# First attention: VectorE takes the maxima before the low part of q, the comparisons before the low part of o, and ScalarE normalises one step later

## The chip, the core and the metric

The kernel runs on one core of a Trainium2 chip. The metric is the device time of one execution in microseconds (us). It is a chain of four layers in one program; the change touches only the first.

## The reference, cut to what matters

Four sub-layers follow one another on x (2 batches of 2048 tokens, 512 wide). The first is a gated cross-attention with 16 heads of 32 over a context of 128 tokens; the second is a layer that runs on the 256 best-scored tokens of each batch.

```
x = x + tanh(g_xattn[0]) * L0_xattn(layernorm(x), ctx, ...)   # first attention: the change is here
x = x + tanh(g_ffn[0])   * L0_ffn(layernorm(x), ...)          # top 256 of 2048 tokens per batch, by x @ w_router
...
q = x @ Wq.T + bq;  att = softmax(q k^T * scale);  out = (att v) @ Wo.T + bo
```

## The kernel before

The first attention (tile names begin with `A_`) goes over 8 tiles of 512 tokens (`n` = 0 to 7). Each tile takes four slots `j` = 0 to 3, one for each group of four heads; a slot is numbered `s` = 4n + j, 0 to 31. Products are made in pairs of a high and a low half, for precision. The order of the work on each engine is written out by hand, and semaphores join the engines.

In slot s, TensorE makes the scores of group s (L982, L984) and the projection of q for the next tile (L914). It then makes the scores from which VectorE takes the maxima of the *next* group (`scores_for_max`, L925), the row sums (L996) and the product with V (`weigh`, L941). The first half of the output projection of the previous tile follows (L603), then the transposed maxima (`turn_maxima`, L932), the transposed router scores and the counts of the ranking (L614, L627), and the second half of the output projection (L603). The next slot's scores need the transposed maxima, copied by ScalarE (`keep_mT`, L825).

In the last slot of a tile (j = 3, while n + 2 < 8) TensorE also transposes x of tile n + 2 in four chunks (L905). ScalarE copies each chunk (`keep_xT`, L817 and L821) and GpSimd makes its low half (`low_x`, L771). The projection of q in the next slot waits for all four. Three conditions of the order matter here:

- In a slot with j = 3, n at least 1 and below 7, the output projection waits for the low half of q of that same slot, since it uses the same bank (`pe.wait_ge(q_ev, QT * (n + 2))` ahead of `project_out`).
- GpSimd's queue has, in such a slot, `low_x` of chunks 0 to 2, then `post_scales` (L515 to L521), which waits for the variance that VectorE's `add_out` (L650 to L657) leaves in this slot, and only then `low_x` of chunk 3 (L771).
- ScalarE's exponentials (L873) stand behind `high_o`, `add_gated` and whatever else the slot still has for ScalarE.

VectorE's slot has: low half of q (`keep_q_low`, L1050), `maxima` (L1089, L1094, L1096), the refined reciprocal of the row sums (L1112, L1114), the division (`divide`, L1101), the router score of a chunk (`score`, L666), the residual sum and its statistics (`add_out`), the low half of the output (`low_o`, L1106), in slots with j = 1 the statistics of x and with j = 2 its layer norm (L1034, L1044), and the comparisons that rank the chunk of six slots ago (`compare`, L678 and L684; the width grows by 128 with each chunk of a batch and starts again at 16).

Of the kernel before, what the change touches and what calls it, by code (L numbers as in the profile page):

```python
# [59 lines left out]
def need(eng, sem, value):  # L60

    if not (isinstance(value, int) and value <= 0):
        eng.wait_ge(sem, value)
# [76 lines left out]
def load_gates(eng, io, cst):  # L140

    for n, name in enumerate(("g_xattn", "g_ffn")):
        eng.dma_start(cst["gates_raw"][:, 2 * n:2 * n + 2],
                      io[name].rearrange("(a n) -> a n", a=1).to_broadcast([P, 2])).then_inc(cst["gates_loaded"], 16)


def make_gates(act, cst):

    act.wait_ge(cst["gates_loaded"], 32)
    act.activation(cst["gates"][:, :], cst["gates_raw"][:, :], ACT.Tanh).then_inc(cst["gates_tanh"], 1)  # L150
# [209 lines left out]
def narrow_attention(nc, io, cst, L, chosen):  # L360
# [8 lines left out]
    SLOTS = GROUPS * STEPS  # L369
    with stage_semaphores(nc, name) as sem, ExitStack() as ctx, ExitStack() as main:  # L370
# [101 lines left out]
        def chunk_at(s, lag):  # L472

            return s - lag if 0 <= s - lag < CHUNKS else None
# [20 lines left out]
        def found_slot(b):  # L495

            return hot_slots(b)[-1] + 1
# [36 lines left out]
        def normalise(act, s):  # L534

            q = chunk_at(s, ROUTE)
            if q is not None:
                (n, c), k = divmod(q, SUB), q + 1
                act.wait_ge(p_sh, 3 * k - 2)
                need(act, fin, k)  # L540
                if c == 0:
                    need(act, stored[n % 2], 32 * (n // 2))
                act.activation(N2[n % 2][:, c, :], R[n % 2][:, c, :], ACT.Identity, bias=shift[:, c:c + 1],
                               scale=rstd2[:, c:c + 1]).then_inc(p_xn, 1)
# [29 lines left out]
        def keep_found(act, s):  # L574

            for b in range(NB):
                if s == found_slot(b):
                    act.wait_ge(found, b + 1)
                    act.activation(idf[:, b, :, :], id_ps, ACT.Copy).then_inc(id_kept, 1)
# [79 lines left out]
        def score(dve, s):  # L659

            q = chunk_at(s, ROUTE)
            if q is not None:
                n, c = divmod(q, SUB)
                need(dve, p_sc, q)
                dve.wait_ge(p_xn, q + 1)
                dve.tensor_tensor_reduce(junk[:, :], N2[n % 2][:, c, :], wr[:, :], 1.0, 0.0, ALU.mult, ALU.add,  # L666
                                         own[:, q:q + 1]).then_inc(p_sc, 1)
# [144 lines left out]
        @block.scalar  # L812
        def _(act):
            def keep_xT(n, c):
                act.wait_ge(x_tr, SUB * n + c + 1)
                need(act, x_lo, SUB * n + c - 1)
                act.activation(xt[c % 2][:, :, :], TX[:, :, :], ACT.Copy).then_inc(x_te, 1)  # L817
                act.wait_ge(x_te, SUB * (n - 1) + c + 1)
                if c == 0:
                    need(act, q_mm, QT * n)  # L820
                act.activation(xh[:, :, c * P:(c + 1) * P], xt[c % 2][:, :, :], ACT.Copy).then_inc(x_hi, 1)  # L821

            def keep_mT(k):
                act.wait_ge(m_tr, k + 1)
                act.activation(mT[:, :], mps, ACT.Copy).then_inc(m_te, 1)  # L825

            def keep_q(n, m, bank=PJ):
                act.wait_ge(q_mm, QT * n + m + 1)
                act.activation(qh[:, m, :], bank[:, :], ACT.Identity, bias=bq[:, m:m + 1]).then_inc(q_hi, 1)

            def guess_rz(k):

                need(act, o_div, k - 1)
                act.wait_ge(z_mm, k)
                act.activation(rz[:, :], ZB[:, :], ACT.Ln).then_inc(z_ln, 1)
                act.wait_ge(z_ln, k)
                act.activation(rz[:, :], rz[:, :], ACT.Exp, scale=-1.0).then_inc(z_ex, 1)

            load_gates(act, io, cst)
            make_gates(act, cst)  # L840
            act.preload_act_table_set("natural_log_exp_and_others")
            act.wait_ge(w_in, 32)
            for k in range(KD):
                act.activation(wqh[:, k, :], wq[:, k, :], ACT.Copy).then_inc(wq_hi, 1)
            for c in range(SUB):
                act.wait_ge(x_tr, c + 1)
                act.activation(xh[:, :, c * P:(c + 1) * P], first_turns[c], ACT.Copy).then_inc(x_hi, 1)
            stage.keep_k(act)
            stage.high_k(act)
            for m in range(QT):  # L850
                keep_q(0, m, first_banks[m % 3])
            for c in range(SUB):
                keep_xT(1, c)
                if c == 2:
                    keep_mT(0)

            def scale_wo(k):
                act.wait_ge(cst["gates_tanh"], 1)
                act.wait_ge(b_in, 48)
                act.activation(wo[:, k, :], wo[:, k, :], ACT.Copy, scale=tg).then_inc(wo_sc, 1)  # L860
                act.wait_ge(wo_sc, k + 1)
                act.activation(woh[:, k, :], wo[:, k, :], ACT.Copy).then_inc(wo_hi, 1)

            def high_o(s):
                act.wait_ge(o_div, s + 1)
                act.activation(oh[s // GROUPS % 2][:, s % GROUPS, :], OB[:, :], ACT.Copy).then_inc(o_hi, 1)

            for s in range(SLOTS):
                n, j = divmod(s, GROUPS)
                last = n == STEPS - 1  # L870
                for g in range(HG):
                    act.wait_ge(s_mm, HG * s + g + 1)
                    act.activation(pr[:, g, :], SC[:, g, :], ACT.Exp, scale=scale).then_inc(s_ex, 1)  # L873
                if not last:
                    keep_q(n + 1, j)
                guess_rz(s + 1)
                normalise(act, s)
                turn_x = j == GROUPS - 1 and n + 2 < STEPS
                if turn_x:
                    keep_xT(n + 2, 0)  # L880
                    keep_xT(n + 2, 1)
                if s + 1 < SLOTS:
                    keep_mT(s + 1)
                keep_row(act, s)
                keep_sums(act, s)
                high_o(s)
                keep_found(act, s)
                if turn_x:
                    keep_xT(n + 2, 2)
                    keep_xT(n + 2, 3)  # L890
                add_gated(act, s)
                if n == 0:
                    scale_wo(j)
# [135 lines left out]
        def _(dve):  # L1029
# [56 lines left out]
            def maxima(k):  # L1086

                dve.wait_ge(m_mm, k + 1)
                dve.tensor_reduce(mx[:, :, :], SC[:, :, :].rearrange("p g (c x) -> p c g x", x=CTX),  # L1089
                                  AX.X, ALU.max).then_inc(m_mx, 1)  # L1090
                dve.wait_ge(m_mx, k + 1)
                need(dve, m_tr, k)
                m = by_slot(m2[:, :, :])
                dve.tensor_copy(m[:, :, :, 0], mx[:, :, :]).then_inc(m_hi, 1)  # L1094
                dve.wait_ge(m_hi, k + 1)
                dve.tensor_tensor(m[:, :, :, 1], mx[:, :, :], m[:, :, :, 0], ALU.subtract).then_inc(m_lo, 1)  # L1096

            def divide(s):

                dve.wait_ge(pv, s + 1)  # L1100
                dve.tensor_tensor(OB[:, :], OB[:, :], rz[:, :], ALU.mult).then_inc(o_div, 1)  # L1101

            def low_o(s):

                dve.wait_ge(o_hi, s + 1)
                dve.tensor_tensor(ol[s // GROUPS % 2][:, s % GROUPS, :], OB[:, :],  # L1106
                                  oh[s // GROUPS % 2][:, s % GROUPS, :].bitcast(F32), ALU.subtract).then_inc(o_ok, 1)
# [16 lines left out]
            for s in range(SLOTS):  # L1124
                n, j = divmod(s, GROUPS)
                last = n == STEPS - 1
                if not last:
                    keep_q_low(n + 1, j)
                if s + 1 < SLOTS:
                    maxima(s + 1)  # L1130
                refine_rz(s + 1)
                dve.wait_ge(z_r, s + 1)
                divide(s)
                score(dve, s)
                add_out(dve, s)
                low_o(s)
                if n + 2 < STEPS and j == 1:
                    ln_stats(n + 2)
                if n + 2 < STEPS and j == 2:
                    ln_apply(n + 2)  # L1140
                compare(dve, s)
                choose(dve, s)

        main.close()  # L1144
# [2023 lines left out]
```

## Time and profile before

| what | value |
| --- | --- |
| median of 3 runs | 1783.61 us (1780.41 to 1787.19) |
| the profiled execution | 1779.8 us, span 1777.9 us |
| mean granted TensorE clock | 0.937 of full speed |
| busy: TensorE, VectorE, ScalarE, GpSimd | 87%, 73%, 51%, 32% of the span |
| first attention | about 20 us to 476 us of the span |

A row of the timeline gives start, duration, engine, line, operation, output and input, and in brackets how long the engine had been idle and what released it.

### The profile page before, as it was taken

The page shows a single profiled execution, that of the slowest core. Times are in us where ns is not written, and L with a number is a line of the kernel's source. Part 1 is how long each engine was busy: PE and PEld are TensorE (multiplying, and loading weights), DVE is VectorE, ACT ScalarE, POOL GpSimd, SP SyncE. Part 2 cuts the span into 40 slices and gives each one's busy share as a digit, 9 for nine tenths or more (in the row PEclk, how much of TensorE's full clock was granted, in tenths as well). Part 3 has the DMA queues.
Part 4 walks back from the last instruction along what each step waited for, and adds up shares of the span by engine and source line. Part 5 has one row for each costly group of instructions (what it writes and reads, how often), then busy time and mean ns, then how long its engine had stood idle before and what let it go on. Part 6 is the DMA issues. An engine that isn't in the chain of part 4 may idle for free. (4 is left out here: it accounts for less than half of the span.)

```text
span 1777.9 us, 25990 instructions
## 1 busy us (share of the span) xinstructions
PE 1544.6 (87%) x9654; PEld 982.3 (55%) x9687; DVE 1300.4 (73%) x2098; ACT 907.4 (51%) x1467; POOL 570.6 (32%) x560
## 2 busy tenths in 40 slices
PE   7788888997678979968999999999997778888887
PEld 5455555554456648745666665666664444554453
DVE  5677788888542546654776775777766599999997
ACT  3556665565544426426334333433433477777774
POOL 3233333123310002113112021112200297777771
PEclk9899999899888889989999999999999999999998
DMA  4112212222722424531020101102011330222111
GB/s 162 48 48 95 95 54 67 72 72 96 277 70 98 180 87 142 201 113 48 1 84 25 60 29 56 60 24 84 1 60 36 120 124 9 69 78 72 67 64 55
DMA packets 73284, 142.36 MB, mean 80 GB/s; under 512 B 8417, under 2 KB 17781, under 8 KB 72906
## 3 DMA queue, kind: packets, MB, share of 16 engines
q1 hardware_dynamic: 71914, 137.55, 22.5%
q0 software_dynamic: 960, 3.15, 0.6%
q8 instruction: 81, 1.33, 0.3%
q14 instruction: 41, 0.34, 0.1%
q10 hardware_dynamic: 288, 0.00, 0.0%
HBM read 97.67 MB, written 43.01 MB: 79 GB/s over the span
## 5 line engine op out<-in xcount | busy, mean ns | idle before, releaser
L2937 POOL TENSOR_TENSOR E_y<-E_y,E_centre 128x1024 f32<-128x1024 f32 x64 | 151.6, 2368 | 6.7 <-ACT E_y L2966 3.7
L1492 ACT ACTIVATE D_oT<-D_OB 128x512 fp32r<-128x512 f32 x64 | 38.3, 599 | 221.0 <-DVE D_OB L1809 221.0
L2929 POOL TENSOR_SCALAR E_centre<-E_hs,E_cw,E_cb 128x512 f32<-128x512 f32 x64 | 108.8, 1700 | 53.4 <-DVE E_hs L3025 53.3
L2825 PE MATMUL E_HP<-E_xT,E_w1q 128*128 128x512 bf16 x482 | 123.9, 398 | 2.4 <-ACT E_xT L2943 0.4
L1781 DVE TENSOR_TENSOR D_q_low<-D_PJ,D_q_high 128x512 fp32r<-128x512 f32 x60 | 41.5, 692 | 97.1 <-ACT D_q_high L1468 97.1
L2850 PE MATMUL E_YT<-ident,E_y 128*128 128x128 f32 x496 | 70.4, 289 | 42.1 <-DVE E_am L3043 38.1
L3034 DVE SCALAR_TENSOR_TENSOR E_y<-E_hs,E_cw,E_y 128x512 f32<-128x512 f32 x128 | 105.4, 862 | 0.0
L2838 PE MATMUL E_OP<-E_w2q,E_yb 128*128 128x512 bf16 x446 | 102.8, 384 | 0.7 <-issue 0.7
L1561 PE MATMUL D_PJ<-D_xT_high,D_wq_high 128*128 128x512 f32 x240 | 101.2, 422 | 0.1
L1561 PE MATMUL D_PJ<-D_xT_high,D_wq_low 128*128 128x512 f32 x240 | 94.7, 395 | 0.0
L1561 PE MATMUL D_PJ<-D_xT_low,D_wq_high 128*128 128x512 f32 x240 | 94.0, 392 | 0.0
L2850 PEld LDWEIGHTS E_YT<-ident,E_y 128*128 128x128 f32 x496 | 60.0, 149 | 58.1 <-issue 41.9
L1569 PE MATMUL D_ZB<-D_wo_high,D_oT 128*128 128x512 f32 x240 | 82.8, 406 | 2.8 <-DVE D_rz L1823 2.8
L2825 PEld LDWEIGHTS E_HP<-E_xT,E_w1q 128*128 128x128 bf16 x512 | 50.3, 102 | 56.4 <-issue 9.7
L1569 PE MATMUL D_PJ<-D_wo_high,D_oT 128*128 128x512 f32 x240 | 80.8, 397 | 0.0
L3025 DVE TENSOR_TENSOR E_hs<-E_HP,E_rs 128x1024 f32<-128x1024 f32 x64 | 77.4, 1209 | 2.7 <-PE E_HP L2825 2.7
L603 PE MATMUL A_TX<-A_wo_high,A_oT 128*128 128x512 f32 x176 | 71.0, 446 | 6.7 <-PEq L1144 6.7
L1791 DVE TENSOR_REDUCE D_mx<-D_SC 128x16 f32<-128x2048 f32 x32 | 73.1, 2284 | 4.1 <-PE D_SC L1582 4.1
L3043 DVE TENSOR_REDUCE E_am<-E_YT 128x4 f32<-128x1024 f32 x62 | 75.2, 1213 | 1.2
L2956 ACT ACTIVATE E_centre<-E_hs,E_cw 128x512 f32<-128x512 f32 x64 | 46.1, 721 | 58.7 <-DVE E_hs L3025 56.8
L914 PE MATMUL A_PJ<-A_xT_high,A_wq_high 128*128 128x512 f32 x120 | 56.6, 472 | 20.6 <-POOL A_xT_low L771 15.4
L1815 DVE TENSOR_TENSOR D_oT<-D_OB,D_oT 128x512 fp32r<-128x512 f32 x64 | 44.2, 691 | 41.0 <-ACT D_oT L1492 41.0
(445 smaller groups left out, 4270.2 us busy)
## 6 DMA issues: line engine op xcount, KB each, us to landing
A_res<-in_x SPq DMA_DIRECT2D x8, 1024.0 KB, 5.4
xn_d<-A_xn SPq DMA_DIRECT2D x8, 1024.0 KB, 4.4
x_d<-A_res SPq DMA_DIRECT2D x8, 1024.0 KB, 4.3
W_raw<-in_w1T SPq DMA_DIRECT2D x16, 512.0 KB, 3.6
W_raw<-in_w2T SPq DMA_DIRECT2D x16, 512.0 KB, 3.8
D_res<-x_d SPq DMA_DIRECT2D x8, 1024.0 KB, 6.0
x_d<-D_res SPq DMA_DIRECT2D x8, 1024.0 KB, 4.5
E_res<-x_d SPq DMA_DIRECT2D x8, 1024.0 KB, 5.5
```

Of the source, the lines that this page charges most:

```text
L603: mm = pe.matmul(out_bank(n, c), o[:, k, c * P:(c + 1) * P], w[:, k, :], start=k == 0 and o is h and w is woh, stop=k == QT - 1 and o is l)
L1561: mm = pe.matmul(bank[:, :], w[:, k, m * P:(m + 1) * P], x[:, k, :], start=k == 0 and x is xh and w is wqh, stop=k == KD - 1 and x is xl)
L1569: mm = pe.matmul(bank, o[i][:, k, c * P:(c + 1) * P], w[half][:, k, :], start=k == 0 and o is oh and w is woh, stop=k == OT - 1 and o is ol)
L1791: dve.tensor_reduce(mx[:, :, :], SC[:, :, :].rearrange("p g (c x) -> p c g x", x=CTX), AX.X, ALU.max).then_inc(m_mx, 1)
L2825: mm = pe.matmul(HP[:, i % 2, e, :], w1q[:, k, m * P:(m + 1) * P], XT[n % 2][:, k, :], start=k == 0, stop=k == KD - 1)
L2838: mm = pe.matmul(out_bank(n, c), yb[:, k, c * P:(c + 1) * P], w2q[:, k, :], start=k == 0, stop=k == MC - 1)
L2850: mm = pe.transpose(turn_bank(i)[:, c, e, :], Y[i // MP % 2][:, 2 * (i % MP) + e, c * P:(c + 1) * P], ident[:, :])
L2929: pool.tensor_scalar(U[i % 2][:, 0, :], hs[i % NBUF][:, 0, 1:TILE + 1], cw[:, 2 * p, 1:2], cb[:, 2 * p:2 * p + 1], ALU.mult, ALU.add).then ...
L2937: pool.tensor_tensor(y, y, U[i % 2][:, :, :], ALU.add).then_inc(t0, 1)
L3025: dve.tensor_tensor(hs[i % NBUF][:, :, 1:TILE + 1], HP[:, i % 2, :, :], RS[n % 2][:, :].rearrange("p (a t) -> p a t", a=1).to_broadcast([P ...
L3034: dve.scalar_tensor_tensor(out=Y[n % 2][:, m, :], in0=hs[i % NBUF][:, e, 2:TILE + 2], scalar=cw[:, m, 2:3], in1=Y[n % 2][:, m, :], op0=ALU ...
L3043: dve.tensor_reduce(am[:, :, i % MP], turn_bank(i).rearrange("p c e x -> p c (e x)"), AX.X, ALU.max, apply_absolute_value=True).then_inc(a ...
```

## The change

Nothing is computed differently; four steps change place within a slot. On VectorE `maxima` comes ahead of `keep_q_low`, and `compare` and `low_o` come directly behind `divide`, ahead of `score` and `add_out`. On ScalarE `normalise` (L543), which stood behind the reciprocal's guess, comes behind `high_o`.

```diff
@@ ScalarE, slot s
                 guess_rz(s + 1)
-                normalise(act, s)
                 turn_x = j == GROUPS - 1 and n + 2 < STEPS
                 if turn_x:
                     keep_xT(n + 2, 0)
...
                 high_o(s)
+                normalise(act, s)
                 keep_found(act, s)
@@ VectorE, slot s
+                if s + 1 < SLOTS:
+                    maxima(s + 1)
                 if not last:
                     keep_q_low(n + 1, j)
-                if s + 1 < SLOTS:
-                    maxima(s + 1)
                 refine_rz(s + 1)
                 dve.wait_ge(z_r, s + 1)
                 divide(s)
+                compare(dve, s)
+                low_o(s)
                 score(dve, s)
                 add_out(dve, s)
-                low_o(s)
...
-                compare(dve, s)
                 choose(dve, s)
```

VectorE's instructions in slot 19 (n = 4, j = 3), before; `A_q_low` is the low half of q, `A_SC` the scores, `A_OB` the output before its projection, `A_oT` its halves, `A_res` the residual, `A_lower` the comparisons:

```order
L1050 SCALAR_TENSOR_TENSOR A_q_low<-A_PJ,A_bq,A_q_high 128x512
L1089 TENSOR_REDUCE A_mx<-A_SC 128x16
...
L1101 TENSOR_TENSOR A_OB<-A_OB,A_rz 128x512
L666 ISA A_junk,A_own_scores<-A_xn_1,A_w_router 128x512
L666 ISA A_own_scores 128x1
L650 TENSOR_TENSOR A_res<-A_PJ,A_res 128x512
L652 BN_STATS A_stats<-A_res 128x6
L655 BN_AGGR A_mv<-A_stats 128x2
L657 TENSOR_SCALAR A_var<-A_mv 128x1
L1106 TENSOR_TENSOR A_oT<-A_OB,A_oT 128x512
L678 SCALAR_TENSOR_TENSOR A_ties_at,A_ties<-A_scores_row,A_own_scores,A_following 128x128
L684 TENSOR_SCALAR A_lower,A_less<-A_scores_row,A_own_scores 128x1792
```

The same slot in the changed kernel:

```order
L1089 TENSOR_REDUCE A_mx<-A_SC 128x16
L1094 CAST A_m<-A_mx 128x16
L1096 TENSOR_TENSOR A_m<-A_mx,A_m 128x16
L1050 SCALAR_TENSOR_TENSOR A_q_low<-A_PJ,A_bq,A_q_high 128x512
...
L1101 TENSOR_TENSOR A_OB<-A_OB,A_rz 128x512
L678 SCALAR_TENSOR_TENSOR A_ties_at,A_ties<-A_scores_row,A_own_scores,A_following 128x128
L684 TENSOR_SCALAR A_lower,A_less<-A_scores_row,A_own_scores 128x1792
L1106 TENSOR_TENSOR A_oT<-A_OB,A_oT 128x512
L666 ISA A_junk,A_own_scores<-A_xn_1,A_w_router 128x512
L666 ISA A_own_scores 128x1
L650 TENSOR_TENSOR A_res<-A_PJ,A_res 128x512
...
L657 TENSOR_SCALAR A_var<-A_mv 128x1
```

The low half of q now stands behind three instructions of the maxima, and the variance (L657) behind both comparisons and the low half of the output.

ScalarE's instructions of slot 20 in the changed kernel, from the reciprocal's guess to the exponentials of the next slot; before, L543 stood between L837 and L825:

```order
L835 ACTIVATE A_rz<-A_ZB 128x512
L837 ACTIVATE A_rz<-A_rz 128x512
L825 ACTIVATE A_mT<-A_SC 128x512
L563 ACTIVATE A_scores_row<-A_SC 128x128
L572 ACTIVATE A_later<-A_SC 128x13
L866 ACTIVATE A_oT<-A_OB 128x512
L543 ACTIVATE A_xn_1<-A_res,A_shift,A_rstd 128x512
L554 ACTIVATE A_res<-A_res,A_offset,A_gain 128x512
L873 ACTIVATE A_probs<-A_SC 128x512 x4
```

The normalisation now stands between the division's result and the exponentials.

## Rows read from the trace of the kernel before

**Rows 1.** Groups of TensorE, 40 to 455 us: busy, mean ns, idle before by releaser.
```profile
L914 PE MATMUL A_PJ<-A_xT_high,A_wq_high 128*128 128x512 f32 x112 | 52.7, 470 | 17.8 <-POOL A_xT_low L771 15.4 <-issue 2.4
...
L932 PE MATMUL A_SC<-identb,A_m 128*128 128x128 bf16 x128 | 13.1, 227 | 22.2 <-DVE A_m L1096 22.2
```

**Rows 2.** Timeline of slots 16 and 17.
```profile
258.95 2.28 DVE L1089 TENSOR_REDUCE A_mx<-A_SC 128x16 f32<-128x2048 f32 x1
...
263.09 0.70 DVE L1101 TENSOR_TENSOR A_OB<-A_OB,A_rz 128x512 f32<-128x512 f32 x1
...
265.13 2.06 ACT L873 ACTIVATE A_probs<-A_SC 128x512 f32<-128x512 f32 x4
...
268.03 0.67 PE L925 MATMUL A_SC<-A_k_high,A_q_high 32*128 32x128 f32 x16
...
268.86 0.75 DVE L1050 SCALAR_TENSOR_TENSOR A_q_low<-A_PJ,A_bq,A_q_high 128x512 fp32r<-128x512 f32 x1 [0.27 <-ACT A_q_high L829]
...
269.53 2.28 DVE L1089 TENSOR_REDUCE A_mx<-A_SC 128x16 f32<-128x2048 f32 x1
...
270.99 0.80 ACT L543 ACTIVATE A_xn<-A_res,A_shift,A_rstd 128x512 f32<-128x512 f32 x1
```

**Rows 3.** Timeline of slot 0, the first tile.
```profile
53.63 0.40 PE L932 MATMUL A_SC<-identb,A_m 128*128 128x128 bf16 x4 [1.88 <-DVE A_m L1096]
...
57.43 2.04 ACT L873 ACTIVATE A_probs<-A_SC 128x512 f32<-128x512 f32 x4
...
60.37 0.67 PE L925 MATMUL A_SC<-A_k_high,A_q_high 32*128 32x128 f32 x16
```

**Rows 4.** Timeline of slot 18 and the start of slot 19.
```profile
285.71 0.40 PE L932 MATMUL A_SC<-identb,A_m 128*128 128x128 bf16 x4 [2.93 <-DVE A_m L1096]
...
292.79 1.38 DVE L678 SCALAR_TENSOR_TENSOR A_ties_at<-A_scores_row,A_own_scores,A_following 128x128 bf16<-128x128 f32 x1
...
295.97 0.74 DVE L1050 SCALAR_TENSOR_TENSOR A_q_low<-A_PJ,A_bq,A_q_high 128x512 fp32r<-128x512 f32 x1
```

**Rows 5.** Timeline of slot 19, up to the projection of slot 20.
```profile
298.31 0.47 PE L603 MATMUL A_PJ<-A_wo_high,A_oT 128*128 128x512 f32 x1
...
298.94 0.94 DVE L1094 CAST A_m<-A_mx 128x16 bf16<-128x16 f32 x1
...
300.20 0.40 PE L932 MATMUL A_SC<-identb,A_m 128*128 128x128 bf16 x4 [0.25 <-DVE A_m L1096]
...
301.13 0.27 ACT L563 ACTIVATE A_scores_row<-A_SC 128x128 f32<-128x128 f32 x1
...
302.91 0.69 DVE L650 TENSOR_TENSOR A_res<-A_PJ,A_res 128x512 f32<-128x512 f32 x1
...
304.58 0.15 DVE L657 TENSOR_SCALAR A_var<-A_mv 128x1 f32<-128x1 f32 x1
...
305.30 0.72 POOL L515 TENSOR_TENSOR A_rstd<-A_var,minus_half 128x1 f32<-128x1 f32 x1
...
305.52 2.07 DVE L684 TENSOR_SCALAR_CACHE_REDUCE A_lower<-A_scores_row,A_own_scores 128x1792 bf16<-128x1792 f32 x1
...
308.37 0.76 PE L914 MATMUL A_PJ<-A_xT_high,A_wq_high 128*128 128x512 f32 x1 [3.14 <-POOL A_xT_low L771]
```

**Rows 6.** Timeline of slot 23: the comparisons at their second smallest width.
```profile
362.82 0.47 DVE L684 TENSOR_SCALAR_CACHE_REDUCE A_lower<-A_scores_row,A_own_scores 128x256 bf16<-128x256 f32 x1
```

**Rows 7.** Stretches of the projection in slots 16 and 20: PEclk is the column before the last two.
```profile
254.40:258.20 3.80, 3.70 (x32) 2.85 (x36) 0.00 (x0) 0.64 (x1) 2.34 (x2) 1.00 0.19 67
308.30:314.80 6.50, 6.43 (x32) 4.77 (x36) 0.22 (x1) 0.69 (x1) 2.28 (x2) 0.53 0.09 34
```

**Rows 8.** Timeline of slot 27 (n = 6, j = 3).
```profile
403.72 0.74 DVE L1050 SCALAR_TENSOR_TENSOR A_q_low<-A_PJ,A_bq,A_q_high 128x512 fp32r<-128x512 f32 x1
...
404.51 0.50 PE L603 MATMUL A_PJ<-A_wo_high,A_oT 128*128 128x512 f32 x1 [1.15 <-DVE A_q_low L1050]
...
407.21 0.40 PE L932 MATMUL A_SC<-identb,A_m 128*128 128x128 bf16 x4 [1.03 <-DVE A_m L1096]
```

## The prediction

> **What bounds the kernel now.** The profiled execution took 1779.8 us. The change touches only the first attention, some 455 us of it, so I read that stretch alone: first the groups of TensorE, then the timeline of each kind of slot.
>
> The groups show what there is to win. TensorE waits 22.2 us in all for VectorE's maxima ahead of the transposes L932, and 15.4 us (about 3.1 us in each of five tiles) for GpSimd's low half of x ahead of the projection L914 [rows 1]. The first is what the change aims at, and 22.2 us its ceiling. The second is what it may lengthen.
>
> Three kinds of slot must be told apart.
>
> *Slots with j = 0 or 1* form a loop. The reader is to see in the timeline that from the division (263.09) to the exponentials (265.13) pass 2.04 us, that the exponentials end at 267.19, and that TensorE takes up its next scores only at 268.03: ScalarE has 0.84 us to spare, TensorE's own queue ends last [rows 2]. The maxima start at 269.53, 10.58 us after those of the slot before (258.95).
>
> *Slots with j = 2* follow the layer norm's statistics. VectorE is late, and TensorE waits 2.93 us for the maxima in slot 18 [rows 4].
>
> *Slots with j = 3* end in a chain: maxima, score row, residual and variance on VectorE (L657 at 304.58), GpSimd's scales (L515 at 305.30), its last low half of x, and the projection at 308.37, for which TensorE waited 3.14 us [rows 5].
>
> **The change, part by part.**
>
> *Maxima ahead of the low half of q.* Before, the maxima wait for q low, which starts at 268.86 and is followed by them 0.67 us later [rows 2]; now they start as soon as the scores are there (268.03 + 0.67, about 268.75). So the maxima come 0.75 us earlier, and low q comes behind them, some 2.8 us later. The division behind both stays where it was, since VectorE does the same work before it.
>
> In the first tile TensorE waits 1.88 us for the maxima and its next scores (60.37) come 0.9 us after the exponentials (57.43 + 2.04) [rows 3]. Moving the first by 0.75 us brings in about 0.65 us a slot before the exponentials decide. Three slots (0 to 2): **-1.9 us**. Bounds: 0 and -2.3 us.
>
> In slots with j = 2, TensorE's wait of 2.93 us shrinks by the same 0.75 us [rows 4]. This head start I carry into the slot with j = 3, which follows, and count it there.
>
> *Normalise behind high o.* It takes 0.80 us [rows 2] and now stands between the division and the exponentials. The loop from division to division becomes 2.04 + 0.80 to the exponentials, 2.06 for them, 0.1 to the next scores, 0.67 for these, 0.07 to the maxima, 4.14 from maxima to division (258.95 to 263.09), and 0.72 for low q, which is now in between: 10.60 us against 10.58 [rows 2]. So what L932 waits no longer (0.2 us) isn't won: ScalarE's spare time is used up. The slots with j = 0 or 1 and those of tile 6 that were shorter than 10.6 us (I count seven, by 0.1 to 0.35 us) come up to it: **+1.0 us**, bounds 0 and +2.
>
> In the last tile there is no projection, and the exponentials stand close behind ScalarE's work; in each of its four slots the 0.80 us may show. Mostly TensorE's scores come later than that. I take **+0.5 us**, bounds 0 and 3.2 (4 x 0.80).
>
> *Slot 27, tile 6.* Here TensorE already waits 1.15 us for low q (403.72 to 404.46) ahead of the output projection (404.51), and then 1.03 us for the maxima (407.21) [rows 8]. Now the maxima start at 403.72 and end 2.75 us later, low q another 0.75 us: 407.25, so the projection starts 2.75 us later. It takes 407.21 - 404.51 - 1.03 = 1.67 us, and L932 comes at 408.95, **+1.7 us**. Bounds: +1.0 and +2.8, the whole delay.
>
> *Slots with j = 3 in tiles 1 to 5.* I work slot 19 out [rows 4, 5]. The maxima take low q's place at 295.97, less 1.0 us: the comparison that took 1.38 us at 292.79 is now done far earlier, beside an idle GpSimd, and should take some 0.4. That is 295.0, a choice. They end after 3.5 us (295.97 + 0.67 to 300.15 before, with a cast of 0.94 us among them) at 298.5, low q at 299.3. The output projection starts at 299.35, not 298.31. Before, it took 300.20 - 298.31 - 0.25 = 1.64 us: L932 at 301.0, +0.8 us. The head start of slot 18 is gone.
>
> The score row, which the comparisons need, came 0.93 + 0.27 us after L932: now 302.2. Comparisons: 2.07 us and 0.3 for the ties: 304.55. Low o and score, each taken at the 0.69 us of L650, which has their shape, 128x512: 305.95. The residual and its statistics, 302.91 to 304.73 before, 1.82 us: 307.8. From L515 to the projection passed 308.37 - 305.30 = 3.07 us: 310.9. The projection is **2.5 us later** than at 308.37. Low o cost 0.7 of this, the comparisons 2.35, and they had slack only of 0.6 (304.73 to 305.30).
>
> In the other four tiles only the comparisons' width differs: 0.47 us at 256 columns [rows 6], 2.07 at 1792 [rows 5], so in between 1.0 at 768 and 1.54 at 1280. By this, slots 15, 11, 7 and 23 lose 2.0, 1.4, 0.9 and 0.9, with slot 19 7.7 us. In slots 7 and 23 VectorE isn't behind, so the head start survives: I take **+5.8 us** in all. Bounds: 2.5 (slot 19 alone) and 7.7.
>
> The cast L1094 took 0.94 us while GpSimd was making low halves of x, for 16 columns [rows 5]. [...]
>
> *The clock.* A projection of 12 matmuls behind the pause of 3.1 us ran in slot 16 at the full 2.4 GHz (granted 1.00; stretch of 3.8 us with the scores) and in slot 20 nearly all at 1.2 GHz (granted 0.53; 6.5 us) [rows 7]. Longer pauses make the second likelier. In slot 16 alone up to 2.7 us are at stake; I take **+1.0 us**, bounds 0 and 8.
>
> **Sum.** -1.9 + 1.0 + 0.5 + 1.7 + 5.8 + 1.0 = +8.1 us: 1787.9 us against 1779.8 of the profiled execution. The median of the runs is 3.8 us above that, which gives 1791.7. I say 1791. A difference under 0.5% (8.9 us) is about what a measurement of this kernel can't tell from none.
>
> The statistics, last in the slot, cost nothing in slots with j = 0 to 2: the variance feeds a normalisation two slots later, and the residual is wanted by TensorE only after its next row sums, over 4 us after L650 before. If that cover went, the price would be the same 2 to 3 us a slot. The stores behind normalise on SP's queue come some 4 us later; the residual they make room for is added a slot and a half later.
>
> **Rivals.**
>
> *Within 0.5%, a small loss*, as above: 1791 us, its own range 1783 to 1792. Chance 0.50.
>
> *The pauses grow and the clock falls with them.* Place: the projections of slots 8, 12, 16, 20 and 24 behind GpSimd, which wait 4.5 to 5.5 us and not 3.1. If each then runs wholly at 1.2 GHz and the clock stays there into the slot, every tile pays 1.5 us more: 7.7 + 5 x 1.5 + the rest (1.3) = +16.5, 1800 us. It decides from about +0.2 us a tile above my sum. For it: four of the five after such a pause already fell in part. Against it: those can't fall twice. [...] Chance 0.42, with the cases where the loops lose more than taken.
>
> *The head start counts everywhere.* The low q isn't waited for since TensorE comes later there than I say, and the variance comes in time. Then 0.75 us in three first slots and five with j = 2, and 0.2 us in some ten others: -8 us, 1776 us. For it: 22.2 us of waiting on maxima. Against it: slot 27 shows the wait for low q already. Half of this case and all beyond it make up 0.08 for faster by over 0.5%; what is left is within 0.5% and counted there.
>
> **Range.** 1780 to 1801: from the lower bounds (with a part of the third case) to the second case. Faster 0.08, same 0.50, slower 0.42.
>
> **What would show it.** In the changed profile TensorE's wait on VectorE ahead of L932 falls from 22.2 to below 15 us; a new wait of L603 on A_q_low appears in slots with j = 3, and of 1 to 4 us in slot 27; TensorE's wait on GpSimd ahead of L914 rises from 15.4 to above 20 us, and GpSimd's L515 there waits on L657. The loops of j = 0 and 1 come to 10.6 us. If L914's wait stays at 15 us, the term of 5.8 is wrong, and the kernel is as fast as before or faster. If L657 is in time but the clock differs, the term of the clock is.

## The result, and the profile after

The changed kernel takes 1805.13 us (median of 4 runs, 1803.19 to 1807.14), the kernel before beside it 1785.4 us (4 runs, 1780.41 to 1787.32): ratio 1.0115, interval 1.009 to 1.014. It is slower by some 20 us, beyond the predicted 1791 us and beyond the range's 1801. The profiled execution took 1803.19 us, against 1779.8.

The groups of TensorE over the first attention in the changed kernel (same stretch and columns as [rows 1]):

```profile
L914 PE MATMUL A_PJ<-A_xT_high,A_wq_high 128*128 128x512 f32 x112 | 52.1, 465 | 21.0 <-POOL A_xT_low L771 19.1 <-issue 1.9
...
L603 PE MATMUL A_PJ<-A_wo_high,A_oT 128*128 128x512 f32 x48 | 22.0, 504 | 11.6 <-DVE A_q_low L1050 11.6
...
L925 PE MATMUL A_SC<-A_k_high,A_q_high 32*128 32x128 f32 x496 | 21.3, 289 | 14.2 <-ACT A_probs L873 14.0
...
L932 PE MATMUL A_SC<-identb,A_m 128*128 128x128 bf16 x128 | 13.9, 236 | 14.6 <-DVE A_m L1096 14.6
```

The row of L925 in the kernel before, where it had not mattered:

```profile
L925 PE MATMUL A_SC<-A_k_high,A_q_high 32*128 32x128 f32 x496 | 22.1, 297 | 6.4 <-ACT A_probs L873 6.4
```

The wait for the maxima fell from 22.2 to 14.6 us. In its place stand 11.6 us of a wait for low q ahead of the output projection (1.1 us before), and 3.7 us more for GpSimd's low x ahead of the projection of q (15.4 to 19.1). TensorE also waits 7.6 us more for the exponentials (6.4 to 14.0). This last wait comes with `normalise`: it is 11.5 to 15.9 us in every experiment that moves it (e4, e6, e8, e10, e11) and 6.4 to 7.0 us in those that don't. What was won at one wait is more than paid at the others.

Slot 19, timeline of the changed kernel, from the maxima to the projection of slot 20 (answers to [rows 5]):

```profile
300.71 2.29 DVE L1089 TENSOR_REDUCE A_mx<-A_SC 128x16 f32<-128x2048 f32 x1
...
303.04 0.71 DVE L1094 CAST A_m<-A_mx 128x16 bf16<-128x16 f32 x1
...
303.78 1.21 DVE L1096 TENSOR_TENSOR A_m<-A_mx,A_m 128x16 bf16<-128x16 f32 x1
...
304.87 0.74 DVE L1050 SCALAR_TENSOR_TENSOR A_q_low<-A_PJ,A_bq,A_q_high 128x512 fp32r<-128x512 f32 x1
...
305.67 0.80 PE L603 MATMUL A_PJ<-A_wo_high,A_oT 128*128 128x512 f32 x1 [2.30 <-DVE A_q_low L1050]
...
306.26 0.63 PE L603 MATMUL A_PJ<-A_wo_low,A_oT 128*128 128x512 f32 x1
...
306.98 0.70 DVE L1101 TENSOR_TENSOR A_OB<-A_OB,A_rz 128x512 f32<-128x512 f32 x1
...
308.40 0.65 PE L932 MATMUL A_SC<-identb,A_m 128*128 128x128 bf16 x4
...
309.88 0.35 DVE L678 SCALAR_TENSOR_TENSOR A_ties_at<-A_scores_row,A_own_scores,A_following 128x128 bf16<-128x128 f32 x1 [2.21 <-ACT A_scores_row L563]
...
310.16 2.08 DVE L684 TENSOR_SCALAR_CACHE_REDUCE A_lower<-A_scores_row,A_own_scores 128x1792 bf16<-128x1792 f32 x1
...
312.33 1.27 POOL L771 TENSOR_TENSOR A_xT_low<-A_xT,A_xT_high 128x512 fp32r<-128x512 f32 x1 [6.20 <-ACT A_xT_high L821]
...
314.08 0.68 DVE L650 TENSOR_TENSOR A_res<-A_PJ,A_res 128x512 f32<-128x512 f32 x1
...
315.98 0.57 POOL L515 TENSOR_TENSOR A_rstd<-A_var,minus_half 128x1 f32<-128x1 f32 x1 [2.37 <-DVE A_var L657]
...
318.89 0.77 PE L914 MATMUL A_PJ<-A_xT_high,A_wq_high 128*128 128x512 f32 x1 [4.74 <-POOL A_xT_low L771]
```

The reader is to see a chain with no slack in it. The output projection stands 2.30 us for low q. It then runs at half clock (0.63 us a matmul, and a granted clock of 0.50 from 305.67 to 308.40, against 0.39 us and 1.00 from 298.31 to 300.20 before) and puts the maxima's transposes, the score row and the comparisons off; VectorE itself stands 2.21 us for that row. Only behind the comparisons comes the residual with its variance, for which GpSimd stands 2.37 us, and TensorE stands 4.74 us for GpSimd. From the maxima to the projection pass 18.2 us; before it was 308.37 - 296.64 = 11.7 (low q ended 0.67 us behind 295.97).

GpSimd's work beside the maxima of that slot:

```profile
301.17 2.51 POOL L805 TENSOR_TENSOR A_res<-A_res,A_bo 128x512 f32<-128x512 f32 x2
303.65 2.48 POOL L771 TENSOR_TENSOR A_xT_low<-A_xT,A_xT_high 128x512 fp32r<-128x512 f32 x2
```

Slot 15 ends in the same way, and the projection behind its pause now runs at half clock too, with its matmuls starting 0.43 us apart. Timeline:

```profile
258.54 0.77 PE L914 MATMUL A_PJ<-A_xT_high,A_wq_high 128*128 128x512 f32 x1 [4.16 <-POOL A_xT_low L771]
259.11 0.63 PE L914 MATMUL A_PJ<-A_xT_high,A_wq_low 128*128 128x512 f32 x1
...
263.93 0.71 PE L925 MATMUL A_SC<-A_k_high,A_q_high 32*128 32x128 f32 x16
```

and that stretch with slot 20's as windows (PEclk is the third number from the end):

```profile
258.54:264.64 6.10, 6.10 (x32) 4.41 (x36) 0.00 (x0) 0.60 (x1) 2.21 (x2) 0.55 0.01 3
318.89:325.60 6.71, 6.71 (x44) 4.21 (x44) 1.57 (x1) 1.19 (x2) 2.19 (x2) 0.76 0.01 2
```

The granted clock of slot 16's projection was 1.00 before and is 0.55 [rows 7]: 5.4 us to the next scores instead of 3.0. Before, its matmuls start 0.23 us apart, and those of slot 20's projection, granted 0.53, 0.43 us apart. The record has shares of full speed, 1.00 and 0.50; they are what the prediction and the expectations call 2.4 and 1.2 GHz. The same two marks before:

```profile
254.50 0.47 PE L914 MATMUL A_PJ<-A_xT_high,A_wq_high 128*128 128x512 f32 x1 [3.07 <-POOL A_xT_low L771]
...
257.46 0.67 PE L925 MATMUL A_SC<-A_k_high,A_q_high 32*128 32x128 f32 x16
```

The end of the slots, which are one block of the program. Behind it comes the first attention's closing part (the last output projections and the rest of the ranking), which starts on TensorE and ScalarE together. Changed kernel:

```profile
467.85 0.15 DVE L657 TENSOR_SCALAR A_var<-A_mv 128x1 f32<-128x1 f32 x1
468.08 0.57 POOL L515 TENSOR_TENSOR A_rstd<-A_var,minus_half 128x1 f32<-128x1 f32 x1 [5.96 <-DVE A_var L657]
...
469.48 2.48 POOL L805 TENSOR_TENSOR A_res<-A_res,A_bo 128x512 f32<-128x512 f32 x2
472.69 0.81 ACT L543 ACTIVATE A_xn<-A_res,A_shift,A_rstd 128x512 f32<-128x512 f32 x1 [7.34 <-PEq L1144]
```

Kernel before:

```profile
448.65 0.70 DVE L1101 TENSOR_TENSOR A_OB<-A_OB,A_rz 128x512 f32<-128x512 f32 x1
...
451.71 0.15 DVE L657 TENSOR_SCALAR A_var<-A_mv 128x1 f32<-128x1 f32 x1
...
453.34 2.48 POOL L805 TENSOR_TENSOR A_res<-A_res,A_bo 128x512 f32<-128x512 f32 x2
...
456.56 0.81 ACT L543 ACTIVATE A_xn<-A_res,A_shift,A_rstd 128x512 f32<-128x512 f32 x1 [5.88 <-PEq L1144]
```

The closing part's first work starts less than 1 us behind GpSimd's last bias (469.48 + 2.48 and 453.34 + 2.48), which stands behind the variance of slot 31. Division to variance took 3.1 us before, and takes 6.2 now (the division is at 461.61): +3.2 us, for TensorE and ScalarE alike.

**Where the 23.4 us of the two profiled executions lie.** The division (L1101) is VectorE's fixed mark in each slot. From its rows, changed less before, with two experiments beside it (below: e5 is the order of before compiled anew, e4 has the edits only in slots with j < 3 of tiles 0 to 6):

| stretch | predicted | changed | e5 | e4 |
| --- | --- | --- | --- | --- |
| division 0 to 3 | -1.9 | -2.2 | +0.4 | -2.0 |
| steps out of slots 3, 7, ... 23 (j = 3) | | +14.9 | -1.7 | +3.5 |
| other steps from 4 to 27 | | -6.2 | -0.6 | -9.6 |
| the last two together | +7.8 | +8.7 | -2.2 | -6.0 |
| 27 to 28 | +1.7 | +1.9 | +0.5 | -1.0 |
| 28 to 31, last tile | +0.5 | +4.3 | +4.1 | +0.3 |
| 31 to the block's end | 0 | +3.2 | +1.6 | +0.6 |
| behind the block, code untouched | 0 | +7.3 | -1.6 | +5.5 |

Single profiles carry several us of their own: with no edit at all the last tile is 4.1 us longer in e5, and the untouched code behind the block differs by -1.6 to +11.4 us among the twelve experiments. So sizes are taken from the timed comparisons, and the profiles say where to look.

### The profile page after: what moved, and what is told of

The parts are those of the page before. It is cut to its first block and busy times, and to the rows that moved or that the text cites. A ratio compares the mean times of both kernels' runs of the same rounds, so it can differ in the third digit from the quotient of the medians.

```text
span 1801.3 us, 26023 instructions
## 1 busy us (share of the span) xinstructions
PE 1558.4 (87%) x9687; PEld 989.1 (55%) x9687; DVE 1296.6 (72%) x2098; ACT 905.4 (50%) x1467; POOL 568.8 (32%) x560
## 5 line engine op out<-in xcount | busy, mean ns | idle before, releaser
L2825 PE MATMUL E_HP<-E_xT,E_w1q 128*128 128x512 bf16 x512 | 129.5, 399 | 0.4 <-ACT E_xT L2943 0.2
L1089 DVE TENSOR_REDUCE A_mx<-A_SC 128x16 f32<-128x2048 f32 x32 | 73.2, 2289 | 65.5 <-PE A_SC L925 65.4
L515 POOL TENSOR_TENSOR A_rstd<-A_var,minus_half 128x1 f32<-128x1 f32 x32 | 21.4, 668 | 187.2 <-DVE A_var L657 187.0
L603 PE MATMUL A_TX<-A_wo_high,A_oT 128*128 128x512 f32 x176 | 69.8, 439 | 8.2 <-PEq L1144 8.2
L914 PE MATMUL A_PJ<-A_xT_high,A_wq_high 128*128 128x512 f32 x120 | 55.8, 465 | 23.4 <-POOL A_xT_low L771 19.1
```

Source lines behind the costliest of these rows:

```text
L2825: mm = pe.matmul(HP[:, i % 2, e, :], w1q[:, k, m * P:(m + 1) * P], XT[n % 2][:, k, :], start=k == 0, stop=k == KD - 1)
```

## The experiments

All ratios are to the kernel before on the same chip, with 95% intervals; the microseconds of a loss or gain are worked out from the ratio. 0.1% is 1.8 us. The experiments' line numbers are shifted by up to three. Their code carries the three edits under conditions; the diffs show what results.

**e1, the maxima alone.**

```diff
+                if s + 1 < SLOTS:
+                    maxima(s + 1)
                 if not last:
                     keep_q_low(n + 1, j)
-                if s + 1 < SLOTS:
-                    maxima(s + 1)
```

> Only the maxima ahead of the low half of q; all else as before. Theory P (a delayed producer in the slots with j = 3): the head start of 0.75 us is kept in slots 0 to 2 and in the slots with j = 2 (about -2.7 and -3 us), and in six slots with j = 3 TensorE waits for low q ahead of the output projection (about 11 us of waiting in the changed kernel), which gives back more than it: the kernel lands between -3 and +6 us of the one before. Theory S (ScalarE's loop: the normalisation between division and exponentials is what costs): without it the head start is pure gain, -5 to -8 us. Theory K (TensorE's clock alone): the wait for low q brings more stretches at 1.2 GHz and +5 us or more.

1790.35 us, 1.0043 [1.0024, 1.0063]. Groups of TensorE:

```profile
L917 PE MATMUL A_PJ<-A_xT_high,A_wq_high 128*128 128x512 f32 x112 | 53.2, 475 | 19.0 <-POOL A_xT_low L771 16.2 <-issue 2.9
L603 PE MATMUL A_PJ<-A_wo_high,A_oT 128*128 128x512 f32 x56 | 26.0, 508 | 14.7 <-DVE A_q_low L1053 14.7
L935 PE MATMUL A_SC<-identb,A_m 128*128 128x128 bf16 x128 | 13.7, 233 | 15.4 <-DVE A_m L1099 15.4
```

The edit that should win costs 7.7 us by itself, a little more than the highest I had named. It brings the wait for low q (14.7 us) and hardly touches that for GpSimd (16.2). It rules out theory S; theory K, which had +5 us or more, fits it as well as P does, and is taken up behind the experiments.

**e2, comparisons and low o alone.**

```diff
                 divide(s)
+                compare(dve, s)
+                low_o(s)
                 score(dve, s)
                 add_out(dve, s)
-                low_o(s)
...
-                compare(dve, s)
```

> Only the comparisons and low o directly behind the division, ahead of the router score and the residual's statistics. Theory P: the variance reaches GpSimd 1 to 3 us later in five slots with j = 3 and in slot 31, where the block's end waits for GpSimd's last bias: 8 to 15 us slower than before, TensorE's wait for GpSimd ahead of the projection above 20 us against 15.4. Theory S: no change, within 2 us. Theory K: about +3 us.

1793.27 us, 1.007 [1.0049, 1.009]. Its group of the projection:

```profile
L917 PE MATMUL A_PJ<-A_xT_high,A_wq_high 128*128 128x512 f32 x112 | 51.7, 462 | 26.0 <-POOL A_xT_low L771 24.1 <-issue 2.0
```

The wait for GpSimd rose from 15.4 to 24.1 us, and nothing else is new. The loss, 12.5 us, is what theory P had (8 to 15). The losses of e1 and e2 add to 1.13%, and the changed kernel's is 1.15%.

**e3, both, with the normalisation at its old place** (e1 and e2's diffs).

> The changed kernel with ScalarE's normalisation put back to its old place. Theory P: the loss stays above 13 of the 20 us, and only the last tile, where the exponentials end the wait, gets back some 4 us. Theory S: most of the loss is gone, within 5 us of the kernel before.

1801.02 us, 1.0085 [1.0054, 1.0116]. Its lower end, 9.6 us, is above the 5 us of theory S, and its upper end holds the whole loss. By the medians moving `normalise` costs 0.3%, which these intervals don't tell from nothing.

**e4, all three edits, but only in slots with j < 3 of tiles 0 to 6.**

```diff
+                if s + 1 < SLOTS and (j < 3 and not last):
+                    maxima(s + 1)
...
+                if j < 3 and not last:
+                    compare(dve, s)
+                    low_o(s)
```

> All three edits in slots with j = 0 to 2 of tiles 0 to 6 only; slots with j = 3 and the last tile as before. Theory P: the losers are gone and the head starts of slots 0 to 2 and of j = 2 are kept, -3 to -6 us against the kernel before, 1778 to 1783 us. Theory S: the loops with j = 0 and 1 still have the normalisation in them and the loss stays in part, +3 us or more. Theory K: within 2 us of before.

1774.89 us, 0.9968 [0.9953, 0.9982]: faster than before. No listed group waits for low q, that for the maxima is 16.6 us, that for GpSimd 16.0. So the whole loss lies in slots with j = 3 and in the last tile.

**e5, no edit**: the order of before, with the conditions all off.

> No edit: the order of the kernel before, compiled once more, for a second profile of it. Every theory: ratio 1.000 within 0.002. What it is for: if TensorE's clock in the last tile is a matter of where the chip's changes of clock happen to fall, this profile may show slots 28 to 31 at another granted clock than 0.94, and the first attention up to 4 us longer or shorter, with nothing changed.

1781.51 us, 1.0008 [0.9991, 1.0025]. Windows of the last tile (division 28 to 31), PEclk third from the end; before:

```profile
419.23:448.65 29.42, 22.98 (x205) 12.65 (x204) 24.94 (x51) 18.46 (x38) 10.57 (x18) 0.94 0.42 143
```

e5:

```profile
417.99:451.46 33.47, 27.06 (x198) 13.67 (x197) 25.09 (x50) 18.04 (x36) 10.55 (x18) 0.80 0.38 127
```

e3, which has two of the edits there:

```profile
429.74:458.55 28.81, 22.39 (x197) 12.13 (x196) 25.07 (x50) 18.20 (x38) 10.08 (x18) 0.94 0.43 145
```

The same instructions in the same order take 29.4 or 33.5 us, with the granted clock at 0.94 or 0.80. The changed kernel's tile (33.7 us at 0.80) is of the second kind. Its +4.3 us are therefore no effect of the edits that this profile can show.

**e6, the changed kernel with slot 31 in the old order** (condition `s < SLOTS - 1` on the comparisons, low o and the normalisation).

> The changed kernel with slot 31 alone in the old order (comparisons behind the statistics, normalisation early). Theory P: the time from the last division to the end of the block falls back by about 3 us (11.0 to 7.8), and the kernel is 3 us faster than the changed one: ratio 1.010 to the one before. Rivals S and K: no change, 1.0115.

1796.57 us, 1.0086 [1.006, 1.0113]. End of the block:

```profile
463.07 0.70 DVE L1104 TENSOR_TENSOR A_OB<-A_OB,A_rz 128x512 f32<-128x512 f32 x1
...
467.03 0.15 DVE L657 TENSOR_SCALAR A_var<-A_mv 128x1 f32<-128x1 f32 x1
...
471.87 0.81 ACT L543 ACTIVATE A_xn<-A_res,A_shift,A_rstd 128x512 f32<-128x512 f32 x1 [6.65 <-PEq L1154]
```

From division to variance pass 4.0 us instead of 6.2, and the block ends 2.3 us sooner behind its last division (8.8 against 11.1). The time agrees with 2 to 5 us, though the intervals of the two kernels overlap.

**e7, the maxima first only where j < 3** (e1 with that condition).

> Only the maxima first, and only in slots with j = 0 to 2; comparisons, low o and normalisation as before. Theory P: the waits on low q are gone and the head starts kept: -2 to -5 us, about as good as all three edits in these slots. Rival C: the comparisons ahead of the statistics are what helped there; then this one is within 1 us of the kernel before.

1776.47 us, 0.9976 [0.9958, 0.9994]. The wait for low q is 1.8 us. The gain is e4's within the intervals, so it is the maxima that win in these slots, and the other two edits add nothing there that the timed runs show. Against e1, the maxima in the seven slots with j = 3 and a next tile cost 0.67%, 12 us: the largest piece of the loss.

**e8, the changed kernel with low q ahead of the maxima where j = 3.**

```diff
-                if s + 1 < SLOTS:
+                if s + 1 < SLOTS and j < 3:
                     maxima(s + 1)
                 if not last:
                     keep_q_low(n + 1, j)
+                if s + 1 < SLOTS and j == 3:
+                    maxima(s + 1)
```

> The changed kernel with low q back ahead of the maxima in the slots with j = 3. Theory P: TensorE's wait for low q (11.6 us) falls to about 1 us, what remains is the late variance and the block's end: 7 to 10 us of the 20 come back, ratio 1.006 to 1.008. Rival (all of the loss is the variance): ratio stays above 1.010.

1789.05 us, 1.004 [1.002, 1.0059]. This one line takes back 0.75%, 13 us, of the changed kernel's loss, somewhat more than I forecast, and agrees with e1 against e7. No listed group waits for low q any more.

**e9, before, with GpSimd's last low half of x ahead of its scales.** Nothing else in GpSimd's queue is altered.

```diff
                     if c == SUB - 1 and ahead:
-                        for i in range(SUB - 1):
+                        for i in range(SUB):
                             low_x(n + 2, i)
                     if n:
                         post_scales(pool, n - 1, c)
-                    if c == SUB - 1 and ahead:
-                        low_x(n + 2, SUB - 1)
```

> The kernel before, with one edit on GpSimd: the low half of x chunk 3 ahead of the scales of the previous tile's last chunk, so that the projection no longer waits behind VectorE's variance. Theory P: in each of five tiles the 1.5 us of the scales leave the path, TensorE's wait for GpSimd falls from 15.4 to about 8 us: 5 to 10 us faster, ratio 0.994 to 0.997. Rival (ScalarE's copies of x end last anyway): within 1 us.

1771.62 us, 0.9925 [0.9906, 0.9945]. The kernel gains 13 us, more than the 5 to 10 I forecast. The wait for GpSimd falls from 15.4 to 8.8 us:

```profile
L912 PE MATMUL A_PJ<-A_xT_high,A_wq_high 128*128 128x512 f32 x112 | 50.8, 453 | 11.2 <-POOL A_xT_low L771 8.8 <-issue 2.4
```

**e10, the changed kernel with the same edit.**

> The same GpSimd edit on the changed kernel. Theory P: the late variance no longer reaches the projection. Of the 20 us lost, what the comparisons cost in slots with j = 3 (some 8 us) and the 5 to 10 us of the edit itself come back; the wait on low q (about 8 us with its slow clock) and the 2.5 us at the block's end stay: ratio 0.999 to 1.005. Rival (the variance isn't what TensorE waits for): the edit brings as much as in the kernel before and no more, ratio about 1.007 to 1.009.

1783.02 us, 0.9998 [0.9984, 1.0013]: with the variance out of the projection's way, the changed order with this edit is as fast as before, and 0.73% slower than e9. The edit brings 1.17% here and 0.75% in e9. The 0.4% between them is close to e12's below, and speaks against the rival.

```profile
L912 PE MATMUL A_PJ<-A_xT_high,A_wq_high 128*128 128x512 f32 x112 | 48.7, 435 | 11.1 <-POOL A_xT_low L771 9.1 <-issue 2.0
...
L603 PE MATMUL A_PJ<-A_wo_high,A_oT 128*128 128x512 f32 x60 | 26.8, 489 | 14.5 <-DVE A_q_low L1048 14.5
```

The wait for GpSimd is that of e9; what stays is the wait for low q.

**e11, e4 and e9 together.**

> The three edits in slots with j = 0 to 2 of tiles 0 to 6, and low x first on GpSimd. If the two gains add up: -6 and -5 to -10 us, ratio 0.990 to 0.994, 1763 to 1770 us. If both use up the same slack: 0.995 to 0.997.

1754.11 us, 0.9837 [0.9816, 0.9858]: 29 us faster than before, more than I forecast and more than the two alone (0.32% and 0.75%).

```profile
L915 PE MATMUL A_PJ<-A_xT_high,A_wq_high 128*128 128x512 f32 x112 | 50.7, 453 | 11.7 <-POOL A_xT_low L771 8.8 <-issue 2.9
...
L933 PE MATMUL A_SC<-identb,A_m 128*128 128x128 bf16 x128 | 12.9, 224 | 14.9 <-DVE A_m L1097 14.9
```

Both waits are short here, and no listed group waits for low q. From division 0 to 31 it takes 370.1 us (before 393.7, e4 385.0, e9 383.2), and by the clock's record TensorE is granted 0.50 for 37.5 us up to division 31, against 64.9 before.

**e12, comparisons and low o moved only where j = 3 in tiles 0 to 6.**

> Only the comparisons and low o ahead of score and statistics, and only in slots with j = 3 of tiles 0 to 6 (not in slot 31). Theory P: this is where the comparisons' move costs; 6 to 11 us slower, ratio 1.0035 to 1.006, against 1.007 with the move everywhere, and TensorE's wait for GpSimd above 20 us. Rival (the cost lies in the last tile or beyond the block): within 2 us of the kernel before.

1791.57 us, 1.0042 [1.0019, 1.0066].

```profile
L917 PE MATMUL A_PJ<-A_xT_high,A_wq_high 128*128 128x512 f32 x112 | 54.1, 483 | 25.0 <-POOL A_xT_low L771 22.6 <-issue 2.4
```

Seven slots make 7.5 us, with the same longer wait for GpSimd (22.6 us) as e2.

## Why the prediction was wrong

The direction was right, though I gave a loss beyond 0.5% less chance (0.42) than one within it (0.50). The two waits were right too: low q behind the maxima holds up the output projection, and the variance behind the comparisons holds up GpSimd and the projection of q. The step that failed is their size in the slots with j = 3: 5.8 us, with 1.7 for slot 27 and 1.0 for the clock 8.5 in all, where the timed runs show 19.5 to 20.5 us. Beside it I put slot 31 at nothing, and it costs 2 to 5. By the timed comparisons the account is:

| piece | from | us |
| --- | --- | --- |
| the edits where j < 3, tiles 0 to 6 | e4 | -5.7 |
| maxima ahead of low q where j = 3 | e1 - e7, changed - e8 | +12 to +13 |
| comparisons and low o first where j = 3 | e12 | +7.5 |
| slot 31 | changed - e6, end of block | +2 to +5 |
| sum | | +16 to +20 |
| measured | | +20.5 |

The table has no row for the edits in slots 28 to 30 and none for `normalise` in slots with j = 3, which no run takes alone.

**The first tile** (-1.9): the profiles don't settle it. Division 0 to 3 shortens by 2.2 us in the changed kernel and by 2.0 in e4, but only by 0.7 in e8 and 0.6 in e11, whose order is the same up to there. The first two steps shorten by 1.2 to 1.4 us in all of them. In the third TensorE is granted 0.50 for 2.6 and 2.8 us in the first two profiles and for 5.2 and 5.3 in the others. e2, without the maxima's edit, shortens by 1.9 as well. So a single profile can't give the size of this term, which lies between -0.6 and -2.2.

**Loops and the normalisation** (+1.0): the mechanism holds. The step from slot 16 to 17 is 10.42 us (10.60 forecast, 10.57 before) and the wait of L932 won there nearly all goes: e1, e7 and e3, which leave `normalise` alone, shorten it by 0.37 us, the changed kernel and e4 by 0.15. The step 5 to 6 grows by 0.9 in the changed kernel, but by 0.8 also in e2 and e3, which leave `normalise` alone and move the comparisons, and not at all in e1 and e7. So that one is the comparisons', which I had in no loop. The longer wait for the exponentials (6.4 to 14.0 us) is the used-up spare time of ScalarE. All small, and not told apart in the timed runs.

**Slot 27** (+1.7): near, 1.9 us, though e6, with the same order there, has 3.7. The projection waited 2.40 us for low q, as worked out, and then ran mostly at half clock (granted 0.55 from 414.00 to 416.50), which I hadn't priced: from its first matmul to L932 it took 2.52 us where I had 1.67.

**Slots with j = 3 in tiles 1 to 5** (+5.8): this is the step that failed, with *the clock* (+1.0) beside it. Both halves came out at about twice the size. My working put the output projection's delay at 0.8 us in each of five slots and 1.7 in slot 27, 5.7 in all, and the timed runs show 12 to 13. It left some 3.7 us for the comparisons and low o, before any head start, and e12 shows 7.5.

Slot 19 was to bring its projection 2.5 us later. Division 18 comes 6.20 us later than before and the projection 10.52: slot 19 makes 4.3 us of it. For slot 15 it is 4.04 - 1.47 = 2.6 us where I had 2.0, and 2.4 more in the projection behind it, granted 0.50 from 258.54 to 263.94. Of the 18.2 us of slot 19's chain I had forecast 15.9 (maxima at 295.0, projection at 310.9). The maxima began 0.5 us sooner, counted from division 18, than I took. The 2.3 us missing are:

- 1.1 us: the output projection to L932 took 308.40 - 305.67 = 2.73 us, and I carried over its old 1.64. Behind its wait of 2.30 us it was granted 0.50, where before it was granted 1.00. I had counted the clock for L914 alone and not for the first matmuls behind the *new* wait.
- 0.6 us: maxima to low q. L1096, on 16 columns, took 1.21 us beside GpSimd's L771 (0.23 us in each row of before), which I had not priced. The same 1.21 to 1.22 us stand in slots 7, 11 and 15.
- 0.45 us: comparisons to residual. The score L666 took 1.39 us, not the 0.69 taken from L650, now that L771 ran beside it. This is slot 19 alone; in all others it took 0.68 or 0.69.
- 0.25 us: L932 to the score row; the small rest is of both signs.

The timeline shows it: L666 began at 312.76 and took 1.39 us while L771 ran from 312.33 to 313.60. In slot 31 of before (at 449.26), with GpSimd idle, it takes 0.68 us. An overlap alone doesn't do it: in slot 19 of before L1096 began at 299.92, beside an L771 from 299.94 to 301.24, and took 0.23 us. I had weighed only the cast, and so missed what moving `score` and L1096 under GpSimd's work would do. The cast itself stayed long, as the sum had taken it: L1094 met L805 (301.17 to 303.68) and took 0.71 us, against 0.94 beside L771 before, where most casts took 0.20.

That the profile's sum up to division 28 (+8.7 us) is near my 7.6 is luck in part: steps such as 10 to 11 are 1.6 us shorter in it, and just as much shorter in e12 and e9, which change nothing there. In the timed runs the j = 3 slots cost 19.5 to 20.5 us, from which the gain of 5.7 goes: 14 to 15 us against my 7.6.

**Slot 31**, in no term: wrong. I wrote that the statistics, last in the slot, cost nothing in slots with j = 0 to 2, and followed j = 3 only where a projection comes next. In slot 31 there is none, but GpSimd's last bias stands behind the same variance and the closing part behind the bias. The profile has 3.2 us for it, and e6 takes 2.3 of them back.

**The last tile** (+0.5): the +4.3 us of the profile are the clock, seen in e5 without an edit and absent in e3 with two.

**The rivals.** That the head start counts everywhere (1776 us) is what e4 shows, 1775 us, once the j = 3 slots and the last tile are left alone. The rival of longer pauses and a falling clock (1800 us) described slot 16 well. Its pauses were too long, though: it had 4.5 to 5.5 us in each of the five tiles, and they are 3.3 to 4.7. Two of the five projections ran wholly at half clock (slots 12 and 16), where one did before (slot 20). A lower clock does go with longer pauses: over the slots of before, the 5.5 us behind TensorE's pauses of 0.9 to 1.5, 1.5 to 2.5 and 2.5 to 3.5 us were granted 0.96, 0.73 and 0.68 on average (10, 9 and 8 pauses). As the whole cause the clock fails, theory K with it. From the start of the profile to division 31 TensorE spends 78.1 us at a granted 0.50 in the changed kernel and 64.9 before, but only 47.8 in e8, which is 7 us slower than before, and 64.4 in e2, which is 12.5 us slower. e10 spends 44.4 us there, fewer than e9 (54.6), and is 13 us slower than e9. The late producers are the cause (e8, e9, e12 each undo or make one), and the half clock adds to some of the waits (2.73 us instead of 1.64 behind that of slot 19). How the 12 to 13 us of low q divide between the wait and the half clock behind it is not shown, since e8 takes both away.

**My signs**: the wait of L932 below 15 us, right (14.6); a new wait of L603 on A_q_low, right (11.6 us); that of L914 above 20 us, nearly (19.1; it is 24.1 in e2, where TensorE isn't held up by low q, so it seems that part of GpSimd's lateness hides behind that wait); loops of 10.6 us, nearly (10.42); a wait of 1 to 4 us for low q in slot 27, right (2.40); L515 waiting on L657, right (2.37 us in slot 19).

**Left open.** What `normalise` costs by itself (0 to 0.3%), why e9 gains 13 us where its wait for GpSimd falls by 6.6, why e4 and e9 add to more than their sum, and whether the 7.3 us behind the block belong to the change in any part. In all twelve experiments the timed difference follows the block's end within 7 us.

## What to carry to other kernels

Before moving a step up, list who is queued behind each step that it passes, in each kind of slot and at the end of the block; a head start that is won in loops is lost if in one kind of slot the passed step feeds the engine that bounds. A condition on the slot (e4) or a change to the consumer's own queue (e9) can be worth more than the move. Price the chain behind a new wait at half clock too (2.73 instead of 1.64 us in slot 19), and look for a time of each moved VectorE instruction beside what GpSimd does at its new place (L666 took 1.39 us instead of 0.68, L1096 1.21 instead of 0.23).

## What the runs showed of the hardware

The granted clock differs between profiles of the same order of work. The last tile is shown above (29.4 and 33.5 us). The second layer, whose code is the same in all kernels, takes 55.7 to 56.7 us in eight profiles, 59.8 in two (e6, e9), 60.8 in e12 and 61.3 in three (e2, e3, e8). Windows of it, PEclk third from the end; before:

```profile
589.90:646.60 56.70, 49.54 (x449) 30.10 (x441) 28.32 (x48) 14.56 (x34) 1.75 (x4) 0.84 0.50 185
```

e8:

```profile
591.60:652.90 61.30, 55.11 (x448) 33.21 (x441) 28.43 (x48) 14.56 (x34) 1.75 (x4) 0.71 0.46 171
```

The wait patterns are alike, and TensorE's clock at 0.84 or 0.71 makes 4.6 us. What decides between them was not found. It means that a difference of under some 5 us in one stage of one profile says nothing by itself.
